# A transformer block over 16 sequences: the slot loop written out, and x loaded one slot later

## What is computed

```python
x = x + attn(layernorm(x))        # 16 heads of 16 features, softmax over 512 keys
x = x + ffn(layernorm(x))         # one linear layer, its input rounded to fp8

qkv = einsum('bsd,ed->bse', x, qkv_w) + qkv_b
scores = einsum('bhqe,bhke->bhqk', q, k) * HD ** -0.5
out = einsum('bhqk,bhke->bhqe', softmax(scores), v)
out = einsum('bsd,ed->bse', out, proj_w) + proj_b          # attn
x_dq = clip(x / input_scale, -448, 448).astype(float8_e4m3fn) * input_scale
out = einsum('bsi,oi->bso', x_dq, weight_fp8 * weight_scale) + bias   # ffn
```

## Time and profile before

| | us |
|---|---|
| median of 3 runs | 1118.22 |
| lowest, highest | 1114.38, 1128.79 |
| the profiled execution | 1118.22 |
| its span, first to last instruction | 1116.4 |
| TensorE busy in the span | 1008.1 (90%) |
| VectorE, ScalarE, GpSimd busy | 834.9, 712.6, 465.6 |
| mean granted TensorE clock | 0.94 of 2.4 GHz |

### The profile page before, as it was taken

The page is one execution under the profiler, slowest core; times in us unless marked ns, Lnnn a source line. Parts: engine busy times, 40 slices in busy tenths (PEclk is TensorE's granted clock), DMA queues, the critical chain, the costliest instruction groups (busy, mean ns, idle before and its releaser), DMA issues.

```text
span 1116.4 us, 18856 instructions
## 1 busy us (share of the span) xinstructions
PE 1008.1 (90%) x5796; PEld 473.8 (42%) x5796; DVE 834.9 (75%) x1186; ACT 712.6 (64%) x1299; POOL 465.6 (42%) x443
## 2 busy tenths in 40 slices
PE   3487999999998999899998999899999999999884
PEld 2243334444544444344444444444444435443333
DVE  3676788888876888777877888868888888788215
ACT  3024777777675777667675777657677777766660
POOL 3121234536261644527172363607355463615241
PEclk9666999999998999899998999989999999999986
DMA  4937281826455281825645083653718073550000
GB/s 135 117 44 92 37 116 20 105 51 100 74 78 98 39 121 28 108 53 77 97 57 99 25 109 60 91 85 49 125 26 107 23 107 49 81 74 21 21 31 27
DMA packets 44308, 79.67 MB, mean 71 GB/s; under 512 B 9904, under 2 KB 13104, under 8 KB 44208
## 3 DMA queue, kind: packets, MB, share of 16 engines
q1 hardware_dynamic: 44208, 78.36, 46.4%
HBM read 18.42 MB, written 8.39 MB: 24 GB/s over the span
## 4 chain that ended last, share of the span: by engine, by line
PE 76%; ACT 10%; issue 6%; DVE 4%; DMA 2%; SPq 1%; POOL 1%; ACTq 0%; DVEq 0%; POOLq 0%
PE ps_t L461 25%; PE ps_o L493 18%; PE ps_m L375 9%; PE ps_s L475 8%; ACT pt L572 6%; PE ps_m L386 5%; PE ps_m L412 4%; PE ps_m L443 3%; ACT parts L609 2%; DVE mx L690 2%; PE ps_m L359 2%; ACT parts L608 1%; SPq L286 1%; DMA ks<-parts 1%; PE ps_m L426 1%
## 5 line engine op out<-in xcount | busy, mean ns | idle before, releaser
L572 ACT ACTIVATE pt<-ps_t 128x512 f32<-128x512 f32 x1024 | 564.0, 600 | 239.8 <-PE ps_t L461 228.6
L690 DVE TENSOR_REDUCE mx<-ps_s 128x2 f32<-128x1024 f32 x512 | 609.6, 1209 | 98.8 <-PE ps_s L475 98.1
L461 PE MATMUL ps_t<-qs,ks 50*128 50x512 f32 x1024 | 435.2, 477 | 49.6 <-ACT pt L572 36.6
L475 PE MATMUL ps_s<-ks,qs 48*128 48x512 f32 x1024 | 395.8, 493 | 22.8 <-DMA ks<-parts 11.8
L461 PEld LDWEIGHTS ps_t<-qs,ks 50*128 50x128 f32 x1024 | 173.5, 190 | 383.5 <-ACT pt L572 302.9
L493 PE MATMUL ps_o<-pt,vt 128*32 128x512 f32 x2048 | 281.3, 622 | 0.3 <-ACT pt L572 0.2
L475 PEld LDWEIGHTS ps_s<-ks,qs 48*128 48x128 f32 x1024 | 160.5, 193 | 50.3 <-DVE mx L690 29.1
L939 POOL TENSOR_TENSOR on<-ot,rden 128x256 f32<-128x256 f32 x63 | 39.5, 628 | 221.7 <-DVE rden L749 221.7
L909 POOL TENSOR_TENSOR xnT_p<-xnT,xnT_p 128x512 fp32r<-128x512 f32 x30 | 38.4, 1280 | 223.6 <-ACT xnT L592 223.6
L745 DVE STREAM_TRANSPOSE ot<-ps_o 128x512 f32<-128x512 f32 x64 | 45.7, 715 | 82.7 <-PE ps_o L493 82.7
L375 PE MATMUL ps_m<-xnT_p,wqkv_p 128*128 128x512 f32 x360 | 103.1, 423 | 1.4 <-POOL xnT_p L909 0.8
(11 more groups left out here) (94 smaller groups left out, 771.4 us busy)
## 6 DMA issues: line engine op xcount, KB each, us to landing
qs<-parts SPq DMA_DIRECT2D x192, 128.0 KB, 6.2
ks<-parts SPq DMA_DIRECT2D x192, 128.0 KB, 6.5
xin<-in_x SPq DMA_DIRECT2D x16, 512.0 KB, 4.0
xres<-in_x SPq DMA_DIRECT2D x16, 512.0 KB, 3.8
out<-h SPq DMA_DIRECT2D x15, 512.0 KB, 8.6
qs<-nmax SPq DMA_DIRECT2D x128, 8.0 KB, 4.5
pt<-in_qkv_wT SPq DMA_DIRECT2D x1, 768.0 KB, 6.2
out<-h SPq DMA_DIRECT2D x2, 256.0 KB, 2.0
```

Source lines behind the costliest of these rows:

```text
L461: nc.tensor.matmul(ps_t[:, g, :], ks[par][rows, slot, keys], qs[par][rows, slot, :], start=True, stop=True).then_inc(st_done, 1)
L475: done = nc.tensor.matmul(ps_s[:, s % 2, g, :], qs[par][rows, slot, queries], ks[par][rows, slot, :], start=True, stop=True)
L572: nc.scalar.activation(pt[n % 2][:, w % 2 + 2 * a, w // 2, :], ps_t[:, a, :], ACT.Exp, scale=SCALE).then_inc(exp_done, 1)
L690: dve.tensor_reduce(mx[:, t, :, s % (STEPS // 2)], ps_s[:, s % 2, :, :], AX_X, ALU.max).then_inc(max_done, 1)
```

## The change

There are two edits. The hardware loop goes: `run_slots` writes all 18 slots out on every engine, and each wait has a constant. And the load of x moves: it was the second item of slot u, for block u+2; it is now the first item of slot u, for block u+1. The extra load of block 1 ahead of the slots goes, since slot 0 now issues it.

```diff
-LOOP_FROM, LOOP_TO = 4, 14
...
-            for u in range(LOOP_FROM):
+            for u in range(NSLOT - 1):
                 slot(u, u % 2, present(u))
                 if u == 0 and prepare:
                     prepare()
-            with eng.Fori(0, (LOOP_TO - LOOP_FROM) // 2) as i:
-                for half in range(2):
-                    slot(i * 2 + (LOOP_FROM + half), half, lambda behind: True)
-            for u in range(LOOP_TO, NSLOT - 1):
-                slot(u, u % 2, present(u))
             finish(B - 1)
...
             def slot(u, par, present):
+                if present(-1):
+                    load(u + 1, 1 - par)
                 if present(2):
                     rows(u - 2, par, 1)
-                if present(-2):
-                    load(u + 2, par)
                 if present(0):
                     stack(u, par, 0)
...
-            load(1, 1)
             run_slots(sp, slot, finish)
```

## The result

| | before | changed |
|---|---|---|
| median, us (4 runs each) | 1121.74 | 1176.40 |
| lowest, highest | 1114.38, 1128.79 | 1175.08, 1178.48 |
| ratio | | 1.049 (95%: 1.041 to 1.057) |
| profiled execution, its span | 1118.22, 1116.4 | 1178.87, 1177.1 |
| mean granted clock of TensorE | 0.94 | 0.926 |

The two profiled executions differ by 60.7 us (the medians by 54.7) where +74 was forecast, and 1176 lies in the range given (1127 to 1216).

A forecast was written before the change was run, and what follows sets the result against it. TensorE's own stream was taken to bound each slot. Late loads add 101.0 us (89.1 in slots 4 to 14, 6.8 in slot 3, 5.1 in slot 1), unrolling saves 26.8: +74 on 1118.22, forecast 1192 us, 80% range 1127 to 1216.

The forecast's parts named there:

- The loop: Slots 4 to 13: writing the loop out removes back-edge gaps and the low clock after them, giving back 26.8 us.
- VectorE's wait: Step 5 of a slot: VectorE waits for the late x behind the store, mean 4.9 us.
- TensorE's gap: Around step 8: TensorE idles for VectorE's maxima, 4.9 less 1.1 us of slack, so 3.8 us per slot.
- The low clock: Steps 8 to 12, after TensorE's gap: clock at 0.50 for 10.2 us, costing 4.3 us per slot.
- the prediction's own factor of 1.8: Time of a group of 8 L493 matmuls: 1.93 us at low clock against 1.06 at full clock.
- Slots 4 to 14: Eleven slots with load and store: 3.8 us gap plus 4.3 us low clock each, 89.1 us added.
- Slots 1 and 2: Slot 1 pays its whole 5.1 us wait for x, no clock cost; in slot 2 the load just makes it.
- The load is not held by the backlog: Rival at step 5: x lands before VectorE needs it, only the loop's gain is left, 1091 us; 7%.
- No low clock: Rival: VectorE waits, but TensorE's clock does not fall after the gap, 1141 us; 16%.
- A short wait of about 3 us: Rival: smaller backlog or earlier store, TensorE's gap 1.9 us, clock falls in some slots only, 1130 us; 8%.
- The loop's stall stays in straight code: Rival: instruction fetches held behind the stack copies keep the loop's cost, 1219 us; 4%.
- the signs that I named: Profile signs: no branch gaps, x waits about 13 times 5 us, mean clock near 0.90, slots 3 to 14 near 69.5 us.

The follow-up runs named there:

- the other queue: Loop written out, load of block u+1 issued by ScalarE on its own queue at step 4, against the kernel before: 1131.27 us, ratio 1.012.
- the filled gap: Changed kernel plus 14 extra matmuls ahead of step 8's scores in slots 3 to 14: 1158.26 us, ratio 1.027 to the kernel before.
- the later reader: Changed kernel with LN1_SUM = (11, 13, 15, 17), so VectorE first reads x at step 11: 1103.83 us, ratio 0.979 to the kernel before.

## Why the prediction was right, and where its sum was off

**The late load decides, and the loop's gain is smaller.** Shown by the two runs with one edit each.

**The loop: 26.8 us.** Its slots gave 25.8 us, its total 16 and 24 us in the two runs with this edit alone (ratios 0.986 and 0.978). The term is right for the slots. What I did not have is that straight slots are not safe from the low clock either: I took two at 61.4 for all, and in one execution five of them were at 63 to 64.4.

**VectorE's wait: 4.9 us.** Over slots 4 to 14 the mean is 5.7. By landing times the load came 1.8 us behind the store on average (1.2 to 2.7) where 1.3 was taken; the store itself took 8.8 on average, against 8.8 and 8.6. That the engines' backlog sets it is shown by the times to landing with the load ahead of the stack copies (4.4 us), and on the other queue (9.1). I had argued from the order of landing; the cause is less the order in a queue than the shared engines.

**TensorE's gap: 3.8 us.** It is 4.3 on average over these slots.

**The low clock: 4.3 us.** This is the term that was mis-sized; it measured 2.4 to 2.7. A slot of 4 to 14 costs 7.0 us more than 61.375 (markers 230.32 to 982.41, 752.1 us for eleven), less 4.3 for the gap: 2.7 us; the filled gap says 2.4. The remaining 0.3 is about what the slots with the later reader cost too. I had taken the length of the low stretch from the back edges, 10.2 us, as if it always came whole and always behind the gap. Here it was 6.8, and 1.4 us of it on average, up to 2.5, passed while TensorE stood anyway. With the prediction's own factor of 1.8 the rest gives an estimate of 5.4 x (1 - 1/1.8) = 2.4.

**The sum.** Slots 4 to 14: 77.0 (89.1 forecast). Slot 3: 7.0 (6.8). Slots 1 and 2: 3.4 (5.1). Less 26.8 against the kernel before gives +60.6, the 60.7 of the spans. That these agree is bookkeeping, since they are sums over the same two traces, and it needs the end of the program to be equally long in both: it is, 133.4 us behind the marker of slot 16, by luck, since the other profiled executions have 133 to 149. Two errors also offset each other: the gap was 0.5 us longer than forecast in each of eleven slots, the low clock cost 1.6 us less.

**The rivals.** The load is not held by the backlog: wrong, it took 10.0 us. No low clock: wrong in the changed kernel, where every slot from 3 to 14 has a clock of 0.95, but true of five of the shorter waits of the other queue's run (slots 3, 7, 8, 11 and 12). A short wait of about 3 us: wrong in the changed kernel, where the shortest in slots 3 to 14 was 5.3. The loop's stall stays in straight code: wrong, no slot has a branch gap. Of the signs that I named, the 0.90 for the mean clock did not come (0.926) and slots 3 to 14 were 67.8 to 68.9 instead of 69.5, for the same reason as the smaller term.

## What to carry to other kernels

Compare a load's lead over its reader with what stands ahead of it on the shared DMA engines, and not with what it takes alone: with 12 copies and a store ahead it needed 10 us, where it had 5, and a second queue did not pass the backlog. A wait in an in-order engine costs what is queued behind it for the bounding engine, so moving the reader by six steps was as good as moving the load. And price an edit together with the other: the back edges that the unrolling removed had been hiding the late load in four slots, so with the late load the unrolling was worth nothing (1177.58 us with the loop, 1176.40 without).

## What the runs showed of the hardware

- The price of a short TensorE gap depends on whether the clock falls, and between 1 and 3 us the size of the gap does not settle that. In one execution (the load on ScalarE's queue) the slots with VectorE waits of 2.54 and 2.77 us kept the clock and grew by 2.1 and 1.9 us, those with 2.57 and 2.59 lost it and grew by 2.8 and 2.9. At 4.0 us the slot grew by 6.3.
- The low stretch is not of one length: 10.2 us behind each 2.0 us gap at the back edges of the kernel before, 6.8 us around the gaps of 4.0 to 5.3 us in the changed kernel, 3.4 or 6.8 us at gaps of 2.4 to 3.2 us with the load ahead of the store only. What of it passes while TensorE stands is not paid again.
- The clock can fall without a TensorE gap of even 1 us: behind 3 us in which it was busy 2.15 to 2.3, three times in one execution and four times in another. A stretch as weak (2.20) also passed without a fall in another execution of the same kernel. Together with the end of the program (133 to 149 us behind the marker of slot 16) this is where two profiled executions of one kernel differed by 16 us. What decides in which slots it falls was not tested.
